# Four layers on one core: row maxima in two halves, and the causal mask of the scores moved from TensorE to GpSimd

## The chip, the core and the metric

The kernel runs on one core of a Trainium2 chip. The metric is the device time of one execution in microseconds; a time of several runs is their median. The core has five engines that take their instructions in order and wait for each other through semaphores: PE is TensorE (matrix products into eight PSUM banks), DVE is VectorE, ACT is ScalarE, POOL is GpSimd, and SP issues transfers.

## The reference, cut to what matters

Sixteen batches of 512 tokens with 128 channels go through four layers, each followed by a residual sum and a layer norm: an RWKV block, a soft decision tree, causal attention with 16 heads of 8 channels, and a mixture of 16 experts. The change is in the attention:

```python
scores = jnp.einsum('bthd,bshd->bhts', q, k) / jnp.sqrt(jnp.float32(dh))
causal = jnp.triu(jnp.full((seq, seq), -jnp.inf, dtype=jnp.float32), k=1)
scores = scores + causal[None, None, :, :]
weights = jax.nn.softmax(scores, axis=-1)
out = jnp.einsum('bhts,bshd->bthd', weights, v).reshape(b, seq, d)
return out @ Wo
```

A token t attends to the keys s up to t. The softmax subtracts each row's maximum before the exponential.

## The kernel before

**Stages.** The batches run through the layers as a pipeline. Each engine has a hand-written list of steps, ORDER, with entries such as `3:score0`: in turn t the step score0 is done for batch t - 3. An engine goes through its list once a turn, so the lists set where every step stands, and nothing reorders them later. One turn brings one batch in and one out, each in another layer; 16 batches and lags of up to 5 make 21 turns, of which the first and last are partly empty.

**Attention of a batch.** The scores are computed twice. First by rows (steps row0 to row39, tokens in the partitions): a unit is 512 columns in one of two banks, S[0] and S[1], and VectorE takes the maxima of it (rowmax, lines 743 and 746). A pair of heads makes five units. After all 40 units four small steps (max_parts, lines 751 to 757) split the negated maxima into three bf16 parts, TensorE turns them (maxT) in bank G, ScalarE copies them (maxT_out), and one transfer (max_rows on SP) puts them as three more rows beside the queries qh. Then come the scores transposed (score0 to score39, keys in the partitions), in the same two banks; their product includes the subtraction of the maximum. ScalarE takes the exponentials into prob (exp0 to exp39), a ring of ten units, and TensorE weighs the values with them (weigh0 to weigh15, four for ten units). pvT_out, back, attend, attT and attn_out end the attention; routing and experts follow. weigh waits for exponentials (semaphore prob), exp of a unit waits until weigh has freed its place in the ring.

**The mask.** Both computations see whole blocks of 128 tokens only as far as the diagonal. On the diagonal block itself a second matmul with the identity adds -1e30 where a key is later than its token: maskb by rows, maskTb in the transposed scores, 64 of each per batch:

```python
mm(to, kh[:, h, i * P:(i + 1) * P], qh[:, h, i * P:T], True, False, skip_group_check=True)
last = mm(to[:, 0:P], identb[:, :], maskTb[:, :], False, True, skip_group_check=True)
```

**Around it.** In the same turn VectorE does the RWKV scans and reciprocals (line 693) of another batch. There, GpSimd has per chunk a weight sum wk (line 386), r_sig (390), gated (395) and rwkv (400), and TensorE the products k, v and r; four read_outs then end in x2 on VectorE (703). GpSimd also has roots of the norms (352 to 360), sums and parts of the rotated heads (rope_sum 418, rest 422, part_lo 428), whose transfers (heads) the next batch's row0 waits for, and half of the gated expert inputs (u, 444). In the trace nearly every matmul has line 925, the helper mm.

Of the kernel before, what the change touches and what calls it, by code (L numbers as in the profile page):

```python
# [23 lines left out]
PARTS = 3  # L24
KROWS = PARTS * PARTS * DH
# [8 lines left out]

LNS = (0, 1, 2, 3, 4, 6, 7)
# [9 lines left out]
    row_ps=UNITS, rowmax=UNITS, max_part=4, maxT_ps=1, maxT=1, max_in=16, score_ps=UNITS, prob=UNITS, pv=16, pvT=2, back_ps=2, pv_inv=2, att=2,  # L45
# [6 lines left out]
        2:heads0 2:heads1 1:shared_bias 0:load 2:max_rows 4:store  # L52
    """,
    pool="""
        2:part_lo0 1:rwkv3 2:rope_sum1 2:rest1 0:root0 2:part_lo1 1:root2 0:x1_gain 0:x1_bias 2:root4 4:root7 3:root6 1:res 0:root1 1:cmr_sig
        1:cmr_sum 3:gate_rest 3:gate_lo 3:u1 1:root3 3:u3 3:u5 0:wk0 3:u7 3:u9 3:u11 0:r_sig0 3:u13 3:u15 0:r_sig1 0:gated0 0:rwkv0 0:r_sig2 0:wk1
        0:wk2 0:gated1 1:root_rms 0:gated2 0:rwkv1 0:r_sig3 0:gated3 1:rope_sum0 0:wk3 1:rest0 0:rwkv2
    """,
    act="""
        2:mix_before4 2:cmk_tanh0 5:norm7 2:cmk_tanh1 4:norm6 2:cmk_tanh2 4:xdT_out 2:cmk_tanh3 4:route_exp 3:values 2:cmr_tanh 1:norm1 3:norm4  # L60
        4:gate_hi 4:gate_mid 4:gT_out 1:mix_before0 1:mix_before1 4:spread1 1:mix_before2 4:spread3 4:spread5 2:norm3 1:k_exp0 4:spread7 2:xbT_out
        1:k_first0 4:spread9 1:r_tanh0 4:spread11 2:gate0 2:gate1 4:spread13 3:vaug 4:spread15 1:r_tanh1 3:maxT_out 1:k_exp1 1:k_exp2 3:exp0 3:exp1
        1:k_first1 3:exp2 3:exp3 1:r_tanh2 3:exp4 3:exp5 3:exp6 3:exp7 2:leafT_out0 3:exp8 3:exp9 2:leafT_out1 3:exp10 1:k_first2 3:exp11 3:exp12
        3:exp13 1:k_exp3 3:exp14 3:exp15 3:exp16 3:exp17 2:norm_rms 3:exp18 3:exp19 2:xcT_out 1:r_tanh3 3:exp20 3:exp21 1:k_first3 3:exp22 3:exp23
        3:exp24 3:exp25 2:part_hi0 3:exp26 3:exp27 3:exp28 2:part_mid0 3:exp29 3:exp30 3:exp31 3:exp32 3:exp33 2:part_hi1 3:exp34 3:exp35 3:pvT_out0
        2:part_mid1 3:exp36 3:exp37 1:weights 3:exp38 3:exp39 0:norm0 3:pvT_out1 1:norm2 3:attT_out 1:mix_before3
    """,
    dve="""
        4:route_probs 3:rowmax10 4:largest0 4:others 3:rowmax11 3:rowmax12 4:largest1 4:gates 3:rowmax13 3:rowmax14 2:y0 3:rowmax15 3:rowmax16 4:u0
        3:rowmax17 2:moments3 4:u2 3:rowmax18 3:rowmax19 1:mix0 1:mix1 1:mix2 4:u4 3:rowmax20 3:rowmax21 1:clamp0 3:rowmax22 4:u6 3:rowmax23  # L70
        3:rowmax24 1:ksum0 3:rowmax25 3:rowmax26 3:rowmax27 4:u8 3:rowmax28 3:rowmax29 1:kv0 3:rowmax30 3:rowmax31 4:u10 3:rowmax32 3:rowmax33
        1:kvsum0 3:rowmax34 4:u12 3:rowmax35 1:clamp1 2:tree0 3:rowmax36 1:wkv0 3:rowmax37 3:rowmax38 4:u14 3:rowmax39 2:tree1 3:max_parts 2:tree2
        2:tree3 1:inverse0 1:kv1 1:clamp2 2:tree4 2:tree5 2:tree6 2:tree7 1:kvsum1 4:yd 1:ksum1 1:wkv1 1:kv2 1:clamp3 1:kvsum2 1:ksum2 1:wkv2 2:yb
        2:moments4 1:inverse1 1:ksum3 1:kv3 1:kvsum3 2:rope_mul0 1:wkv3 2:rope_mul1 1:inverse2 1:inverse3 2:rope_mul2 2:rope_mul3 0:moments0
        4:moments7 1:x2 1:weights 1:moments2 3:attend0 3:attend1 2:rowmax0 2:rowmax1 0:moments1 2:rowmax2 3:yc 1:mix3 3:moments6 1:mix4 2:rowmax3
# [10 lines left out]
        1:cmk0 1:cmk1 2:row5 2:row6 1:cmk2 2:row7 2:row8 3:xdT 1:cmk3 3:centroids 2:row9 1:cmr 2:row10 3:shared 1:cmv0 2:row11 2:row12 1:cmv1 2:row13
        1:cmv2 2:row14 1:cmv3 2:row15 3:gT 2:row16 0:xnT 3:gb0 2:row17 3:biases 3:gb1 3:expert0 3:gb2 2:row18 2:row19 3:gb3 3:expert1 3:gb4 2:row20
        2:row21 3:expert2 0:v0 0:k0 3:gb5 2:row22 3:expert3 3:gb6 2:row23 2:row24 3:expert4 3:gb7 2:row25 1:xbT 2:row26 3:gb8 0:r0 2:row27 3:expert5
        2:row28 2:row29 3:gb9 3:expert6 2:row30 2:row31 3:gb10 1:gates0 2:row32 3:expert7 2:row33 3:gb11 2:row34
# [4 lines left out]
def build(nc: bass.Bass, a, out):  # L94
    with ExitStack() as ctx:
# [52 lines left out]
        maskb, maskTb = sb("maskb", [P, P], BF16), sb("maskTb", [P, P], BF16)  # L148
# [146 lines left out]
        def _(sp):  # L295
# [39 lines left out]
            run("sp", {"load": lambda b: load(b + 1) if b + 1 < B else None, **each("heads", 2, spread_heads), "max_rows": spread_maxima, "store": store, "shared_bias": shared_bias})  # L335
            until(sp, B - 1, "stored")


        @block.gpsimd
        def _(pool):  # L340
# [576 lines left out]
        def _(pe):  # L917
# [317 lines left out]
```

## Time and profile before

| | before |
|---|---|
| median of 3 runs | 1767.74 us (1767.66 to 1773.95) |
| the profiled execution, its own time | 1774.35 us |
| its span, first to last instruction | 1772.6 us |
| mean granted TensorE clock | 0.962 of full speed |
| busy in the span: PE, DVE, ACT, POOL | 90%, 82%, 57%, 51% |
| busy in a steady turn of 98.70 us: PE, DVE, ACT, POOL | 95.81, 89.99, 61.98, 55.40 us |

The clock is full from 226 us to 1650 us after the trace's first event and changes between its two levels before and after. A busy PE is not PE at its peak, since matmuls overlap: the step from the start of one matmul to the start of the next tells what one costs in a row of them.

### The profile page before, as it was taken

How to read it: one execution, taken by the hardware profiler on the slowest of the kernel's cores; microseconds unless marked ns; L12 is line 12 of the kernel's file. 1: busy time of each engine (PE TensorE's matmuls, PEld its weight loads, DVE VectorE, ACT ScalarE, POOL GpSimd, SP SyncE). 2: the span in 40 equal slices, each digit the busy share in tenths (PEclk: the TensorE clock that was granted, in tenths of full speed). 3: DMA queues.
4: the chain of work that ended last, by engine and by line, in shares of the span. 5: the costliest groups of instructions: out<-in, count | busy, mean ns of one | idle time of the engine just before them, and what ended most of it. 6: DMA issues, size and time to landing. Idle time of an engine off the chain costs nothing.

```text
span 1772.6 us, 33600 instructions
## 1 busy us (share of the span) xinstructions
PE 1599.3 (90%) x12064; PEld 1073.9 (61%) x12141; DVE 1460.7 (82%) x3386; ACT 1004.2 (57%) x1998; POOL 898.4 (51%) x1120
## 2 busy tenths in 40 slices
PE   4367799999999999999999999999999999998876
PEld 1235357576666757576666767575757667574635
DVE  5677879899898989898998989898998989783702
ACT  3233474857656574757566574747566575736251
POOL 6435274646456464746555464736465564632202
PEclk9687899999999999999999999999999999999887
DMA  4001010100102020101102010101101020101000
GB/s 108 0 6 54 8 55 9 36 25 22 47 9 61 8 55 14 46 16 30 40 10 59 8 54 15 54 8 39 30 17 52 8 55 8 55 9 50 12 7 7
DMA packets 66921, 53.35 MB, mean 30 GB/s; under 512 B 8322, under 2 KB 65474, under 8 KB 66754
## 3 DMA queue, kind: packets, MB, share of 16 engines
q1 hardware_dynamic: 65602, 50.41, 10.3%
q8 instruction: 96, 1.57, 0.4%
q10 hardware_dynamic: 1152, 0.79, 0.1%
q14 instruction: 71, 0.58, 0.1%
HBM read 8.44 MB, written 4.19 MB: 7 GB/s over the span
## 4 chain that ended last, share of the span: by engine, by line
PE 69%; DVE 22%; ACT 3%; issue 3%; DMA 1%; POOL 1%; SPq 0%; ACTq 0%; DVEq 0%; POOLq 0%
PE bank L925 65%; DVE rmax L746 6%; PE bank L921 4%; DVE stats L645 2%; DVE rmax L743 2%; DVE mixed L654 1%; DVE inner L654 1%; DVE prob L826 1%; DVE mv L650 1%; DVE wkb L693 1%; DMA qh<-maxT 1%; ACT rth L498 1%; ACT prob L498 1%; ACT pvT L498 1%; DVE xc L776 1%
## 5 line engine op out<-in xcount | busy, mean ns | idle before, releaser
L498 ACT ACTIVATE prob<-bank 128x512 f32<-128x512 f32 x640 | 353.8, 595 | 122.3 <-PE bank L925 114.5
L746 DVE TENSOR_REDUCE rmax<-bank 128x1 f32<-128x512 f32 (+2 forms) x768 | 353.0, 502 | 11.8 <-PE bank L925 11.3
L444 POOL TENSOR_TENSOR prob<-xdT,spread 128x512 f32<-128x512 f32 x128 | 172.7, 1349 | 251.9 <-ACT spread L498 208.7
L925 PE MATMUL bank<-kh,qh 72*128 72x512 bf16 (+3 forms) x1024 | 257.0, 305 | 20.6 <-DVE rmax L746 11.0
L925 PE MATMUL bank<-wexpT,prob 128*128 128x128 f32 x2048 | 271.6, 280 | 1.0
L925 PEld LDWEIGHTS bank<-wexpT,prob 128*128 128x128 f32 x2048 | 254.9, 194 | 19.8 <-issue 12.4
L925 PE MATMUL bank<-qh,kh 75*128 75x512 bf16 (+3 forms) x1024 | 246.2, 304 | 10.9 <-ACT prob L498 5.7
L498 ACT ACTIVATE spread<-bank 128x512 f32<-128x512 f32 x128 | 76.4, 597 | 255.5 <-PE bank L925 127.7
L693 DVE RECIPROCAL wkb<-wkb 128x512 f32<-128x512 f32 x64 | 211.6, 3327 | 0.0
L925 PE MATMUL bank<-maskb,identb 128*128 128x128 bf16 x1024 | 191.8, 222 | 0.0
L925 PE MATMUL bank<-maskTb,identb 128*128 128x128 bf16 x1024 | 190.8, 221 | 0.0
L925 PEld LDWEIGHTS bank<-qh,kh 75*128 75x128 bf16 x1024 | 100.1, 98 | 148.5 <-ACT prob L498 95.3
L925 PE MATMUL bank<-prob,vaug 128*32 128x512 f32 (+3 forms) x2048 | 175.8, 445 | 0.0
L925 PEld LDWEIGHTS bank<-kh,qh 72*128 72x128 bf16 x1024 | 102.6, 100 | 90.9 <-DVE rmax L746 44.2
L386 POOL TENSOR_TENSOR wkb<-wkb,ksum 128x512 f32<-128x512 f32 x64 | 88.6, 1384 | 133.9 <-DVE ksum L680 74.0
L498 ACT ACTIVATE rth<-bank 128x512 f32<-128x512 f32 x128 | 76.1, 594 | 87.4 <-PE bank L925 73.5
L925 PEld LDWEIGHTS bank<-maskb,identb 128*128 128x128 bf16 x1024 | 101.9, 100 | 32.9 <-issue 13.7
L925 PEld LDWEIGHTS bank<-maskTb,identb 128*128 128x128 bf16 x1024 | 101.2, 99 | 29.5 <-issue 26.8
L356 POOL TENSOR_TENSOR rstd<-var,exponent 128x4 f32<-128x4 f32 x112 | 113.5, 1013 | 1.3
L826 DVE TENSOR_TENSOR prob<-xdT,bank 128x512 f32<-128x512 f32 x128 | 86.5, 676 | 27.1 <-PE bank L925 23.9
L400 POOL TENSOR_TENSOR inner<-rth,wkb 128x512 f32<-128x512 f32 x64 | 95.4, 1490 | 15.4 <-DVE wkb L693 13.6
L390 POOL TENSOR_SCALAR rth<-rth 128x512 f32<-128x512 f32 x64 | 50.6, 790 | 88.0 <-ACT rth L498 88.0
(210 smaller groups left out, 3288.1 us busy)
## 6 DMA issues: line engine op xcount, KB each, us to landing
qh<-part SPq DMA_DIRECT2D x288, 64.0 KB
kh<-part SPq DMA_DIRECT2D x288, 64.0 KB
x<-in_L_attn_x_dram SPq DMA_DIRECT2D x16, 256.0 KB, 3.0
out_dram<-yo SPq DMA_DIRECT2D x16, 256.0 KB, 3.2
qh<-maxT SPq DMA_DIRECT2D x16, 48.0 KB
wk<-in_L_attn_tm_Wk_dram ACTq DMA_DIRECT2D x1, 256.0 KB, 5.9
wv<-in_L_attn_tm_Wv_dram ACTq DMA_DIRECT2D x1, 256.0 KB, 6.2
wr<-in_L_attn_tm_Wr_dram ACTq DMA_DIRECT2D x1, 256.0 KB, 6.4
```

Of the source, the lines that this page charges most:

```text
L356: raised(pool.tensor_tensor(rstd[:, n, :], var[:, n, :], exponent[:, :], ALU.pow), f"root{n}")
L386: raised(pool.tensor_tensor(wkb[:, c % 2, :], wkb[:, c % 2, :], ksum[:, c % 2, 0:T], ALU.add), "wk")
L390: raised(pool.tensor_scalar(rth[:, c % 2, :], rth[:, c % 2, :], 0.5, 0.5, ALU.mult, ALU.add), "r_sig")
L400: raised(pool.tensor_tensor(inner[:, c, :], rth[:, c % 2, :], wkb[:, c % 2, :], ALU.mult), "rwkv")
L444: raised(pool.tensor_tensor(ug[:, e % 4, :], xdT[:, :], spread[e // 2 % 2][:, :], ALU.mult), "ug_side")
L498: raised(act.activation(dst, src, func, **kw), signal)
L645: last = dve.bn_stats(stats[:, n, j, :], t[:, j, :])
L693: raised(dve.reciprocal(wkb[:, c % 2, :], wkb[:, c % 2, :]), "wk_inv")
L746: last = dve.tensor_reduce(rmax[:, j, h:h + 1], S[n % 2][:, col:col + (j + 1) * P], AX_X, ALU.max)
L826: raised(dve.tensor_tensor(ug[:, e % 4, :], xdT[:, :], G, ALU.mult), "ug")
L921: last = pe.transpose(bk[:, j * P:(j + 1) * P], t[:, j, :], ident[:, :])
L925: return pe.matmul(out_, w, x, start=start, stop=stop, **kw)
```

## The change

The masks on the transposed scores go, with maskTb. The exponentials of the diagonal blocks are taken of unmasked scores, and a new GpSimd step, cut, overwrites those of later keys with zeros in place: for each pair of heads one AFFINE_SELECT over four diagonal blocks, one over two, and, after the pair's fifth unit, one over two more. weigh waits for cut instead of prob. The maxima are split, turned, copied and transferred in two halves of eight heads. The first half borrows S[0] after row unit 24; row unit 26 waits for its copy. score20 to score39 wait for the second half, which uses G as before. The order lists of all engines are new.

```diff
+HALF_MAX = PARTS * NH // 2
+FREED_FOR_MAXIMA = 24
...
-        2:heads0 2:heads1 1:shared_bias 0:load 2:max_rows 4:store
+        2:heads0 2:heads1 1:shared_bias 0:load 2:max_rows0 2:max_rows1 4:store
...
+        2:cut10 2:cut11 1:rope_sum1 0:gated3 0:rwkv2 0:rwkv3 1:rest1 2:cut12
...
-            def spread_maxima(b):
-                until(sp, b, "maxT")
-                sp.dma_start(qh[KROWS:KALL, :, :], maxT[:, :]).then_inc(sems["max_in"], 16)
+            def spread_maxima(b, z):
+                until(sp, b, "maxT", z + 1)
+                sp.dma_start(qh[KROWS:KALL, z * NH // 2:(z + 1) * NH // 2, :], maxT[:, :]).then_inc(sems["max_in"], 16)
...
-                if e == NE - 1 and b + 1 < B:
-                    until(pool, b + 1, "max_part")
...
+            def cut_later_keys(b, k):
+
+                pair, last = k // 2, k % 2
+                first = 5 * (pair % 2)
+                until(pool, b, "prob", 5 * pair + 4 + last)
+                diagonals = [prob[:, first + 4, :].rearrange("p (n s) -> p n s", n=2)[:, :, 0:P]] if last else [prob[:, first:first + 4, 0:P], prob[:, first + 1:first + 4:2, 3 * P:]]
+                for t in diagonals:
+                    raised(pool.affine_select(out=t, in_=t, compare_op=ALU.is_ge, fill=0.0, base=0, pattern=[[0, t.shape[1]], [1, P]], channel_multiplier=-1), "cut")
...
-            def max_parts(b):
-                until(dve, b, "rowmax")
+            def max_parts(b, z):
+
+                heads = slice(z * NH // 2, (z + 1) * NH // 2)
+                to, of, left, done = max_part[z], rmax[:, :, heads], max_rest[:, :, heads], 4 * z
+                until(dve, b, "rowmax", (z + 1) * UNITS // 2)
+                if z == 0:
+                    until(dve, b - 1, "maxT_ps")
...
-                if n >= 2:
+                if n == FREED_FOR_MAXIMA + 2:
+                    until(pe, b, "maxT", 1)
+                elif n >= 2:
                     until(pe, b, "rowmax", n - 1)
...
+                for j in range(J):
+                    last = mm((S[0], G)[z][:, j * P:(j + 1) * P], max_cols[z][:, j * HALF_MAX:j * HALF_MAX + P], identb[:, :])
                 raised(last, "maxT_ps")
...
-                if n == 0:
-                    until(pe, b, "max_in")
+                if n in (0, UNITS // 2):
+                    until(pe, b, "max_in", 16 if n == 0 else 32)
...
-                    mm(to, kh[:, h, i * P:(i + 1) * P], qh[:, h, i * P:T], True, False, skip_group_check=True)
-                    last = mm(to[:, 0:P], identb[:, :], maskTb[:, :], False, True, skip_group_check=True)
+                    last = mm(to, kh[:, h, i * P:(i + 1) * P], qh[:, h, i * P:T], skip_group_check=True)
                 raised(last, "score_ps")
...
-                until(pe, b, "prob", 10 * g + (8, 9, 9, 10)[step])
+                until(pe, b, "cut", 6 * g + (5, 5, 5, 6)[step])
```

On TensorE, around the first score, a steady turn of the kernel before has the following; the turning of the maxima, a product k and three more experts stand right ahead of it. wexpT are expert products, qh with kh the scores, mixed with wr an RWKV product.

```order
L925 MATMUL bank<-wexpT,prob 128x128 [waits s_ug_side]
L925 MATMUL bank<-wexpT,prob 128x128 x3
L925 MATMUL bank<-qh,kh 128x512 [waits s_rowmax,s_max_in]
L925 MATMUL bank<-maskTb,identb 128x128
L925 MATMUL bank<-qh,kh 128x384
L925 MATMUL bank<-maskTb,identb 128x128
L925 MATMUL bank<-qh,kh 128x128
L925 MATMUL bank<-maskTb,identb 128x128
L925 MATMUL bank<-mixed,wr 128x512 [waits s_k_min]
L925 MATMUL bank<-qh,kh 128x512 [waits s_prob]
L925 MATMUL bank<-maskTb,identb 128x128
```

The changed kernel has there:

```order
L942 MATMUL bank<-wexpT,prob 128x128 [waits s_ug_side]
L942 MATMUL bank<-wexpT,prob 128x128 x3
L942 MATMUL bank<-qh,kh 128x512 [waits s_rowmax,s_max_in]
L942 MATMUL bank<-qh,kh 128x384
L942 MATMUL bank<-qh,kh 128x128
L938 MATMUL bank<-ident,tree 128x128 [waits s_gate,s_leaf]
L938 MATMUL bank<-ident,tree 128x128 x3
L942 MATMUL bank<-qh,kh 128x512 [waits s_prob]
```

The masks are gone. The turning of the maxima no longer stands between rows and scores: its first half stands in the row part, behind row25, and its second behind score5.

On GpSimd, in the middle of the scoring part, the kernel before has these steps one behind the other (inner is rwkv, rth is r_sig or gated, tree the rotary sums and rests, part the last part of the heads):

```order
L400 TENSOR_TENSOR inner<-rth,wkb 128x512 [waits s_gated,s_wk_inv]
L390 TENSOR_SCALAR rth<-rth 128x512 [waits s_r_tanh]
L395 TENSOR_TENSOR rth<-rth,kvb 128x512 [waits s_r_sig,s_wkv]
L418 TENSOR_TENSOR tree<-tree 128x512 [waits s_rope_mul]
L386 TENSOR_TENSOR wkb<-wkb,ksum 128x512 [waits s_k_first,s_k_sum]
L422 TENSOR_TENSOR tree<-tree,part 128x512 [waits s_part1]
```

The changed kernel has from the second rwkv on:

```order
L405 TENSOR_TENSOR inner<-rth,wkb 128x512 [waits s_gated,s_wk_inv]
L456 AFFINE_SELECT prob<-prob 128x2x128 [waits s_prob]
L456 AFFINE_SELECT prob<-prob 128x4x128 [waits s_prob]
L456 AFFINE_SELECT prob<-prob 128x2x128
L456 AFFINE_SELECT prob<-prob 128x2x128 [waits s_prob]
L400 TENSOR_TENSOR rth<-rth,kvb 128x512 [waits s_r_sig,s_wkv]
L423 TENSOR_TENSOR tree<-tree 128x512 [waits s_rope_mul]
L391 TENSOR_TENSOR wkb<-wkb,ksum 128x512 [waits s_k_first,s_k_sum]
L427 TENSOR_TENSOR tree<-tree,part 128x512 [waits s_part1]
```

The 24 selects of a batch stand in this queue, each waiting for exponentials, with all that follows behind them.

## Rows read from the trace of the kernel before

**Rows 1.** The page, part 1: busy us, share, instructions.
```profile
PE 1599.3 (90%) x12064; PEld 1073.9 (61%) x12141; DVE 1460.7 (82%) x3386; ACT 1004.2 (57%) x1998; POOL 898.4 (51%) x1120
```

**Rows 2.** Timeline of ScalarE: start us, us, what, [idle before <-releaser].
```profile
800.15 0.59 ACT L498 ACTIVATE maxT<-bank 48x512 bf16<-48x512 f32 x1 [0.52 <-PE bank L925]
...
898.85 0.59 ACT L498 ACTIVATE maxT<-bank 48x512 bf16<-48x512 f32 x1 [0.52 <-PE bank L925]
```

**Rows 3.** Tile maxT: count, ns min/median/max, first and last start.
```profile
L498 ACT ACTIVATE maxT<-bank x16: 590/590/591, 205.0 to 1678.1; 48x512 bf16<-48x512 f32 x16
```

**Rows 4.** Windows of a turn: window: length, busy PE, PEld, DVE, ACT, POOL.
```profile
800.20:898.90 98.70, 95.81 (x753) 65.45 (x757) 89.99 (x210) 61.98 (x124) 55.40 (x69) 1.00 0.11 31
844.20:871.60 27.40, 24.84 (x190) 18.57 (x192) 25.18 (x81) 17.94 (x39) 13.43 (x24) 1.00 0.20 55
871.60:903.20 31.60, 31.38 (x224) 24.62 (x227) 30.73 (x62) 11.51 (x22) 15.99 (x17) 1.00 0.04 11
903.20:942.90 39.70, 39.61 (x339) 22.30 (x338) 34.09 (x68) 32.52 (x64) 25.96 (x29) 1.00 0.12 31
```

**Rows 5.** The chain, 838 to 875 us: start, us, what.
```profile
845.56 0.27 DVE pvi L765
...
871.65 3.49 PE bank L925 x25
```

**Rows 6.** Timeline of VectorE around x2 and attend.
```profile
840.72 0.69 DVE L703 TENSOR_TENSOR x<-x,bank 128x512 f32<-128x512 f32 x1 [3.50 <-PE bank L925]
841.44 0.87 DVE L645 BATCH_NORM_STATS2 stats<-x 128x6 f32<-128x128 f32 x4
...
843.12 0.69 DVE L770 TENSOR_TENSOR att<-bank,pvi 128x128 f32<-128x128 f32 x3
845.56 0.26 DVE L765 RECIPROCAL pvi<-bank 128x16 f32<-128x16 f32 x1 [1.75 <-PE bank L921]
```

**Rows 7.** Waits of VectorE in the turn: total us, times, longest.
```profile
DVE tree L737 <- PE bank L925: 0.6, 2, 0.4
```

**Rows 8.** Tile maskTb.
```profile
L925 PE MATMUL bank<-maskTb,identb x1024: 218/220/315, 209.7 to 1714.3; 128*128 128x128 bf16 x171
...
L473 POOL TENSOR_SCALAR_AFFINE_SELECT maskTb<-maskTb x1: 292/292/292, 20.1 to 20.1; 128x128 bf16<-128x128 bf16 x1
```

**Rows 9.** Timeline of TensorE, a score with its mask and the next.
```profile
903.43 0.22 PE L925 MATMUL bank<-maskTb,identb 128*128 128x128 bf16 x1
903.50 0.33 PE L925 MATMUL bank<-qh,kh 75*128 75x384 bf16 x1
```

**Rows 10.** Tile max_cols in the turn.
```profile
L757 DVE TENSOR_TENSOR max_cols<-max_rest,max_cols x1: 225/225/225, 897.6 to 897.6; 128x64 bf16<-128x64 f32 x1
```

**Rows 11.** Tile rth.
```profile
L390 POOL TENSOR_SCALAR rth<-rth x64: 608/717/1537, 30.2 to 1515.5; 128x512 f32<-128x512 f32 x64
```

**Rows 12.** Groups of GpSimd, 903.2 to 942.9 us: busy us, mean ns, idle before.
```profile
L386 POOL TENSOR_TENSOR wkb<-wkb,ksum 128x512 f32<-128x512 f32 x3 | 4.3, 1431 | 4.0 <-DVE ksum L680 4.0
L395 POOL TENSOR_TENSOR rth<-rth,kvb 128x512 f32<-128x512 f32 x3 | 3.8, 1273 | 1.3 <-DVE kvb L654 1.3
...
L356 POOL TENSOR_TENSOR rstd<-var,exponent 128x4 f32<-128x4 f32 x2 | 2.0, 1016 | 0.0
...
L360 POOL TENSOR_TENSOR shift<-minus,rstd 128x4 f32<-128x4 f32 x1 | 0.2, 203 | 0.1
```

**Rows 13.** Timeline of ScalarE, the exponentials 3 and 4 and the last two.
```profile
905.37 1.08 ACT L498 ACTIVATE prob<-bank 128x512 f32<-128x512 f32 x2
...
940.22 1.08 ACT L498 ACTIVATE prob<-bank 128x512 f32<-128x512 f32 x2 [0.91 <-PE bank L925]
```

**Rows 14.** Timeline of GpSimd, the last rwkv of a turn.
```profile
932.52 1.28 POOL L400 TENSOR_TENSOR inner<-rth,wkb 128x512 f32<-128x512 f32 x1 [0.20 <-DVE wkb L693]
```

**Rows 15.** Timeline of TensorE, the first read_out and the score behind it.
```profile
934.62 1.11 PE L925 MATMUL bank<-wo,inner 128*128 128x128 f32 x8
935.56 0.38 PE L925 MATMUL bank<-qh,kh 75*128 75x512 bf16 x1
```

More of the change, by code:

```diff
@@ L61 @@
[L61 to L64, printed above, removed]
@@ L72 @@
[L72 to L75, printed above, removed]
@@ L86 @@
[L86 to L89, printed above, removed]
+        3:score1 2:leafT0 3:score2 2:leafT1 3:score3 3:score4 1:r2 3:score5 3:maxT1 3:score6 1:v2 3:score7 3:score8 2:leaf_sum 3:score9 3:score10
@@ L90 @@
+        0:k1 3:expert6 2:row30 0:v1 2:row31 3:gb10 3:expert7 2:row32 2:row33 3:gb11 3:expert8 3:gb12 0:r1 3:expert9 2:row34 2:row35 3:gb13 3:expert10
+        3:gb14 3:expert11 0:k2 2:row36 2:row37 3:gb15 3:expert12 2:row38 2:row39 3:expert13 3:expert14 3:expert15 2:score0
     """,
@@ L183, in build @@
         rmax, max_rest = sb("rmax", [P, J, NH]), sb("max_rest", [P, J, NH])
-        max_cols, gate_cols = (sb(n, [P, (J - 1) * PARTS * NH + P], BF16) for n in ("max_cols", "gate_cols"))
-        max_part, gate_part = (t[:, 0:J * PARTS * NH].rearrange("p (j i h) -> p j i h", j=J, i=PARTS) for t in (max_cols, gate_cols))
-        maxT = sb("maxT", [PARTS * NH, T], BF16)
+        gate_cols = sb("gate_cols", [P, (J - 1) * PARTS * NH + P], BF16)
+        gate_part = gate_cols[:, 0:J * PARTS * NH].rearrange("p (j i h) -> p j i h", j=J, i=PARTS)
+        max_cols = [sb(f"max_cols{z}", [P, (J - 1) * HALF_MAX + P], BF16) for z in range(2)]
+        max_part = [t[:, 0:J * HALF_MAX].rearrange("p (j i h) -> p j i h", j=J, i=PARTS) for t in max_cols]
+        maxT = sb("maxT", [HALF_MAX, T], BF16)
         pvT = attT = sb("pvT", [P, T])
@@ L334, in _ @@
             sp.wait_ge(setup["kh_ones"], 4)
-            run("sp", {"load": lambda b: load(b + 1) if b + 1 < B else None, **each("heads", 2, spread_heads), "max_rows": spread_maxima, "store": store, "shared_bias": shared_bias})
+            run("sp", {"load": lambda b: load(b + 1) if b + 1 < B else None, **each("heads", 2, spread_heads), **each("max_rows", 2, spread_maxima), "store": store, "shared_bias": shared_bias})
             until(sp, B - 1, "stored")
@@ L598, in _ @@
                 "values": take_values, "vaug": place_values, **each("part_hi", 2, first_part), **each("part_mid", 2, second_part),
-                "maxT_out": lambda b: move(b, maxT[:, :], G[0:PARTS * NH, :], "maxT_ps", "maxT"),
+                **each("maxT_out", 2, lambda b, z: move(b, maxT[:, :], (S[0], G)[z][0:HALF_MAX, :], "maxT_ps", "maxT", z + 1, freed=[("max_in", 16 * (2 * b + z))])),
                 **each("exp", UNITS, score), **each("pvT_out", 2, weighed),
@@ L838, in _ @@
                 **each("tree", DEPTH, tree), "yb": add_tree, "moments4": lambda b: (until(dve, b, "yb"), moments(b, 4, yb)),
-                **each("rope_mul", 4, rope_product), **each("rowmax", UNITS, row_maxima), "max_parts": max_parts, **each("attend", 2, attended),
+                **each("rope_mul", 4, rope_product), **each("rowmax", UNITS, row_maxima), **each("max_parts", 2, max_parts), **each("attend", 2, attended),
                 "yc": add_attention, "moments6": lambda b: (until(dve, b, "yc"), moments(b, 6, yc[b % 2])),
@@ L1176, in _ @@
                 "xcT": turn_in, **each("rope", 4, rope_product), "attn_v": attention_values,
-                **each("row", UNITS, row_scores), "maxT": turn_maxima, **each("score", UNITS, scores), **each("weigh", 16, weigh),
+                **each("row", UNITS, row_scores), **each("maxT", 2, turn_maxima), **each("score", UNITS, scores), **each("weigh", 16, weigh),
                 **each("back", 2, turn_back), "attT": turn_attention, "attn_out": attention_out, "xdT": turn_experts, "centroids": centroids,
```

91 lines of the change are left out of this document (51 added, 40 removed).

## The prediction

> **What bounds the kernel now.** I read the page first, then the period of the program, then one period stage by stage, then the chain and the waits. The page gives busy shares of 90% for TensorE, 82% for VectorE, 57% for ScalarE and 51% for GpSimd [rows 1]; as averages over filling and draining they name no bound. The copy of the maxima (maxT) occurs once a batch, at 800.15 and 898.85 us, so a steady turn takes 98.70 us [rows 2]; from first to last copy there are 15 turns in 1473.1 us, 98.2 on average [rows 3]. In that turn TensorE is busy 95.81 us and VectorE 89.99 [rows 4]: two engines near their limit, each with its own tight stage. In the maxima part after the attention's tail (844.2 to 871.6) TensorE is busy for 24.84 of 27.40 us; from there on it has almost no gap (31.38 of 31.60, 39.61 of 39.70) [rows 4]. The chain says the same: it is VectorE's from 845.56 to 871.6, TensorE's from there on [rows 5], and TensorE's alone until the end of the attention.
>
> VectorE's idle time in a turn is short and named: 3.5 us before x2 (line 703), waiting for read_out on TensorE, 1.8 before the second half of attend (line 765) [rows 6], and six waits of 0.2 to 0.6 us, 1.9 together; those before the rotary products make the largest entry (0.6 for two) [rows 7]. That is 7.2 us; so of 98.70 us VectorE is occupied for 91.5, its short gaps between dependent instructions included. **This is the number that decides**: whatever TensorE is relieved of, VectorE leaves at most 7.2 us of a turn to win.
>
> **The change, part by part.** *The masks on the scores go.* 64 matmuls of 128 columns a batch (1024 in all). The profile puts 220 ns on each [rows 8], but they are pipelined: in the scoring part the next matmul starts 0.07 us after a mask's start (903.43 to 903.50) [rows 9], and 0.06 at most of the others. 64 x 0.06 = 3.8 us a turn. In the scoring part TensorE has no gap [rows 4], so all of it is on TensorE's path there: 98.70 - 3.8 = 94.9 us, were TensorE alone to decide. Bounds: nothing (if VectorE holds the turn) and 3.8.
>
> *The maxima in two halves.* VectorE does eight small steps instead of four. The old ones take up to 0.225 us on 64 elements [rows 10]; the new ones have 32 and take, I estimate, 0.18 with the wait for the one before: eight make 1.45, the four old ones 0.9. I add 0.6 us a turn (bounds 0.2 and 0.9). One more copy of 0.59 us on ScalarE and one more transfer of half the size lie beside other work: ScalarE is busy for 62 of 98.70 us [rows 4]. What the halves give is freedom: the first scores no longer wait for the chain row39, maximum, four steps, turning, copy, transfer. But TensorE did experts and projections in that gap and did not stand still (31.38 of 31.60) [rows 4], so I book no gain of its own, only that the work can stand elsewhere. Row score 26 now waits for the first half's copy, as their bank is borrowed; two other units of work stand ahead of it, and I book nothing (at worst one copy and its hops, 1 us).
>
> *GpSimd's selects.* For each pair of heads there are three: 512, 256 and 256 elements, 24 a batch. The trace has AFFINE_SELECT on 128 elements only: 292 ns [rows 8]. A plain GpSimd pass, TENSOR_SCALAR on 512, takes 608 at its best [rows 11], and a small step of 4 elements 0.20 us [rows 12]. From 0.20 to 0.608 is 0.8 ns an element, and with that 128 elements give 0.30, just the 292 seen: I take 0.6, 0.4 and 0.4, so 1.4 us a pair and 11 us a turn. Upper bound: 292 for every block of 128, 2.34 a pair, 18.7 a turn. The lower bound is that of 512 at the rate alone, 9 us. The Trainium skill (GPSIMD Engine Reference, section 3.1) has about 1.8 cycles an element for a tight loop, 769 ns on 512; by it, as an estimate, a pair takes 1.54 us and a turn 12.3. No run here shows that figure yet.
>
> *Where the selects stand.* They belong to the scoring part, where GpSimd is busy for 25.96 of 39.70 us [rows 4]. In the new order one weight sum (1.43), one gating (1.27) and one root (a power of 1.02 and three small steps of 0.20) leave this part [rows 12], which leaves 21.6; with 11 it is 32.6 us. The selects can start after the first four exponentials (906.45) and end after the last (941.3): 34.9 us [rows 13]. So GpSimd fits, with 2 us to spare, in a queue that takes its steps in order. The weighing on TensorE now waits for the select: after the last exponential that it needs, two selects (1.0 us) instead of none. TensorE has two to three more scores in hand there, and ScalarE needs 0.54 a score; what is left of the wait, 0.2 to 0.7 us at four places a turn, falls on a TensorE that has just won 3.8 us. I count it as spent slack, not as path. Also behind GpSimd: the last part of the rotated heads (part_lo1) stands behind the select of the seventh pair now, and the next batch's row scores wait for its transfers.
>
> One rule weighs against this step. The row first: the same TENSOR_SCALAR on GpSimd takes 608 ns at best, 717 in the median and up to 1537 [rows 11]. The Trainium skill (SBUF — State Buffer, section Who interferes with whom) says that a VectorE instruction with two inputs in SBUF and a GpSimd instruction that reads SBUF exclude each other on a shared port for a whole instruction. The spread agrees with it. Without the rule the selects cost 11 us; at the median's excess over the best case, 0.11 us each, 24 of them cost 2.6 more, 13.6: then GpSimd needs 35.2 of 34.9 us, no spare time at all, but less over it than the 2.4 us that I find below.
>
> *VectorE after the change.* Occupied: 91.5 + 0.6 = 92.1. Which waits stay? The one before x2: from the end of the last reciprocal the chain is weighted product on GpSimd (1.28 [rows 14]), four read_outs on TensorE (0.94 each, by the start of the first and of the score behind it [rows 15]), three scores between them (0.7, at 0.22 to 0.24 without masks) and 0.4 of hops: 6.1 us. VectorE has beside it a set of moments and attend's first half, which today, after x2, run from 841.44 to 843.81: 2.4 us [rows 6]. 3.7 us stay, about as before. The wait before attend's second half shrinks: two sets of moments (1.2 each), x2 (0.69) and one row maximum now lie beside weighing, copy and turning (3.9), so 0.2 stays. Of the 1.9 us of short waits 1.7 is for TensorE, which is up to 3.8 us earlier; I leave 0.3. Turn: 92.1 + 3.7 + 0.2 + 0.3 = 96.3 us, 2.4 less than now. TensorE needs 94.9 and fits.
>
> **Sum.** 15 turns x 2.4 = 36 us. Ends: in the last batch nothing hides the selects (four waits of up to 1 us), while the masks leave a scoring part in which ScalarE waits for TensorE; I set these against each other. The profiled execution's own time is 1774.35 (span 1772.6); less 36 it is 1738. The median of the runs shown is 1767.74, 6.6 below the profiled one, so I predict **1732 us**. By the Trainium skill's rate above (12.3 us of selects) the sum would be the same, since 21.6 + 12.3 still fits into 34.9.
>
> **Rivals.**
> *More comes back (0.18).* If read_outs follow each other with no score between and the short waits go, the turn is 92.1 + 3.0 = 95.1, close to TensorE's 94.9: 15 x 3.6 = 54, 1714 us. For it: the order is new everywhere. Against: the x2 chain alone needs 5.4 us.
> *VectorE keeps it (0.15).* The short waits stay and x2's too: 92.1 + 3.7 + 0.2 + 1.9 = 97.9, so 15 x 0.8 = 12: 1756 us. For it: in the maxima part VectorE has the chain [rows 5], and the masks removed were not there.
> *GpSimd becomes the bound: slower (0.22).* It decides once its scoring part is over by more than the 2.4 us otherwise won: 21.6 + selects > 34.9 + 2.4, selects above 15.7 us a turn, 0.65 each on average. At 18.7 the part is 40.3 against 34.9: 5.4 too long, the turn 96.3 + 5.4 = 101.7, 15 x 3.0 = 45 slower: 1813. At 15.7 it is even, and so it is with selects of 0.55 and the 2.6 of waiting above. Late selects then show as TensorE waiting at the weighing, late transfers of the heads, and row scores that wait for them. For it: no select of this shape in the trace; against: 292 ns fits the line of a plain pass.
> The forecast itself has 0.45.
>
> **Chances and range.** A measurement of this kernel tells about 0.5% (9 us) from no change: below 1759 is faster, above 1777 slower. Forecast and first rival are faster (0.63), of the second (1756, at the edge) a third: 0.68. The rest of it (0.10) and a fifth of the third are the same: 0.14. Slower: 0.18. For 8 in 10 I cut half of the first rival's lower side and the upper half of the third: 1703 to 1785. The forecast alone would have 1721 to 1748.
>
> **What would show it.** Right: no mask matmuls in the scoring part, AFFINE_SELECT of 512 at about 0.6 us and of 256 at 0.4; a turn, copy to copy of the second half, of 96 to 97 us; VectorE's x2 wait still 3 to 4 us and its wait before line 765 gone; TensorE's busy share of a turn lower by 3 to 4 points, with its gaps at the weighing. Wrong: selects of 0.9 us or more, GpSimd without gaps from the first to the last select, and row scores waiting for the heads' transfers; or a VectorE with hardly any idle time, in a turn below 95.

## The result, and the profile after

The changed kernel takes **1823.72 us** (median of 4 runs, 1820.75 to 1826.93) beside 1769.91 us of the kernel before on the same chip: ratio 1.030, 95% interval 1.028 to 1.032. It is slower by 3%; the prediction was 1732 us, and its range ended at 1785.

The page, busy time per engine and the granted clock, answers to [rows 1]:

```profile
PE 1593.4 (87%) x11104; PEld 1030.0 (56%) x11181; DVE 1483.5 (81%) x3450; ACT 1019.7 (56%) x2014; POOL 1094.6 (60%) x1503
...
PEclk9788899999999999999999999999999999998867
```

TensorE has lost the instructions that it was meant to lose, and its share fell; GpSimd has 196 us more. The tile view of the maxima's copies (from 925 to 1036 us; two second halves and one first) gives the turn, and the windows of one turn show where it grew; the columns are those of [rows 4]:

```profile
L510 ACT ACTIVATE maxT<-bank x3: 573/573/587, 929.6 to 1031.7; 24x512 bf16<-24x512 f32 x3
```
```profile
864.70:920.40 55.70, 53.68 (x388) 40.65 (x394) 54.12 (x150) 31.94 (x65) 27.57 (x40) 1.00 0.10 27
920.40:923.30 2.90, 2.90 (x29) 2.89 (x27) 2.87 (x7) 0.63 (x1) 1.37 (x2) 1.00 0.00 0
923.30:963.80 40.50, 35.99 (x248) 17.94 (x247) 32.16 (x48) 30.53 (x58) 36.49 (x45) 0.96 0.12 32
963.80:966.50 2.70, 2.60 (x36) 1.01 (x35) 2.35 (x13) 0.08 (x2) 2.46 (x7) 1.00 0.36 100
```

From copy to copy it is 102.1 us, where 98.70 stood [rows 2]. The four windows are the row scores, what lies between them and the scores, the scores (first score to last exponential), and the tail. The first three of them in the kernel before, cut at the same steps:

```profile
845.40:895.40 50.00, 47.91 (x360) 36.53 (x363) 48.34 (x126) 25.81 (x54) 23.47 (x35) 1.00 0.10 29
895.40:903.20 7.80, 7.80 (x55) 6.13 (x53) 7.56 (x17) 2.45 (x5) 4.75 (x5) 1.00 0.15 42
903.20:941.30 38.10, 38.10 (x315) 21.68 (x318) 32.89 (x61) 30.98 (x60) 24.64 (x26) 1.00 0.10 28
```

The row part with what lies behind it grew by 0.8 us (57.8 to 58.6), the scoring part by 2.4 (38.1 to 40.5). In the scoring part GpSimd is busy for 36.49 of 40.50 us, where it had 24.64 of 38.10; TensorE, which had no gap there, now has 4.5 us of them. How GpSimd goes through this part, its timeline shows:

```profile
925.97 1.27 POOL L400 TENSOR_TENSOR rth<-rth,kvb 128x512 f32<-128x512 f32 x1 [4.20 <-DVE kvb L666]
927.20 1.09 POOL L391 TENSOR_TENSOR wkb<-wkb,ksum 128x512 f32<-128x512 f32 x1
928.25 3.23 POOL L456 TENSOR_SCALAR_AFFINE_SELECT prob<-prob 128x512 f32<-128x512 f32 x5
...
946.81 1.16 POOL L427 TENSOR_TENSOR tree<-tree,part 128x512 f32<-128x512 f32 x1
947.92 2.28 POOL L456 TENSOR_SCALAR_AFFINE_SELECT prob<-prob 128x512 f32<-128x512 f32 x3
950.17 0.61 POOL L395 TENSOR_SCALAR rth<-rth 128x512 f32<-128x512 f32 x1
950.75 1.58 POOL L433 TENSOR_TENSOR part<-tree,part 128x512 bf16<-128x512 f32 x1
952.30 1.35 POOL L456 TENSOR_SCALAR_AFFINE_SELECT prob<-prob 128x512 f32<-128x512 f32 x3
```

GpSimd waits 4.2 us for VectorE's kvb, 2.7 of them inside the part. That wait is over at 925.97, before the first four exponentials are done (926.42) and any select could start. From then on it runs with almost no gap to the end of the part: a row without a bracket shows no wait. The timelines of ScalarE and TensorE at the third weighing show what such a queue does to them:

```profile
949.08 2.17 ACT L510 ACTIVATE prob<-bank 128x512 f32<-128x512 f32 x4
954.54 0.60 ACT L510 ACTIVATE prob<-bank 128x512 f32<-128x512 f32 x1 [3.29 <-PE bank L942]
```
```profile
950.81 0.88 PE L942 MATMUL bank<-qh,kh 75*128 75x512 bf16 x3 [0.20 <-ACT prob L510]
953.34 2.75 PE L942 MATMUL bank<-prob,vaug 128*32 128x512 f32 x24 [1.65 <-POOL prob L456]
```

The exponentials end at 951.25. Their select stands in the queue behind a pass on r_sig and a part of the rotated heads, starts at 952.30, and TensorE's weighing starts at 953.34, after a wait of 1.65 us. The scores of the next two units are done by 951.70, but there are ten slots for exponentials, and the next ten cannot run ahead of the weighing that frees them: ScalarE has nothing to do for 3.29 us and goes on at 954.54, when the first of these weighings has ended (954.41). Exponential, select, weighing, next exponential is a closed ring.

The groups of GpSimd by shape give the selects' durations (busy us, mean ns, idle before), and the tile view their spread (min/median/max):

```profile
L456 POOL TENSOR_SCALAR_AFFINE_SELECT prob<-prob 128x256 f32<-128x256 f32 x256 | 139.5, 558 | 7.3 <-ACT prob L510 7.3
...
L456 POOL TENSOR_SCALAR_AFFINE_SELECT prob<-prob 128x512 f32<-128x512 f32 x128 | 100.7, 787 | 44.1 <-ACT prob L510 43.8
```
```profile
L456 POOL TENSOR_SCALAR_AFFINE_SELECT prob<-prob x384: 398/410/1565, 212.3 to 1764.4; 128x256 f32<-128x256 f32 x128, 128x512 f32<-128x512 f32 x64
```

The spread has two levels, and the single records of the trace tell them apart. 314 of the 384 selects take 0.63 to 0.65 or 0.40 to 0.42 us. The other 70, the same five of 24 in fourteen batches, take 1.08 to 1.57, and they make up nearly all that the means have over the least. Each of these 70 starts while a VectorE instruction with two inputs in SBUF is running (a scan in 56 cases) and ends after it; none of the 314 starts so. One of the 70, and the scan:

```profile
937.70 1.33 POOL L456 TENSOR_SCALAR_AFFINE_SELECT prob<-prob 128x256 f32<-128x256 f32 x1
```
```profile
937.53 1.30 DVE L697 TENSOR_TENSOR_SCAN kvsum<-decay,kvb 128x512 f32<-128x512 f32 x1
```

### The profile page after: what moved, and what is told of

Read it like the earlier page. It is cut to its first block, busy times and chain, and to the rows that moved or that the text cites. A ratio compares the mean times of both kernels' runs of the same rounds, so it can differ in the third digit from the quotient of the medians.

```text
span 1824.8 us, 32237 instructions
## 1 busy us (share of the span) xinstructions
PE 1593.4 (87%) x11104; PEld 1030.0 (56%) x11181; DVE 1483.5 (81%) x3450; ACT 1019.7 (56%) x2014; POOL 1094.6 (60%) x1503
## 4 chain that ended last, share of the span: by engine, by line
PE 42%; DVE 20%; POOL 17%; issue 11%; ACT 7%; DMA 1%; SPq 1%; ACTq 0%; POOLq 0%; DVEq 0%
PE bank L942 41%; POOL prob L456 7%; DVE rmax L758 6%; ACT prob L510 3%; DVE stats L657 2%; POOL inner L405 2%; DVE inner L666 2%; PE bank L938 1%; POOL rth L395 1%; DVE mixed L666 1%; POOL rth L400 1%; POOL tree L423 1%; POOL wkb L391 1%; DVE mv L662 1%; DVE prob L843 1%
## 5 line engine op out<-in xcount | busy, mean ns | idle before, releaser
L942 PEld LDWEIGHTS bank<-wexpT,prob 128*128 128x128 f32 x2048 | 264.9, 193 | 24.0 <-issue 18.7
L942 PE MATMUL bank<-wexpT,prob 128*128 128x128 f32 x2048 | 267.3, 276 | 1.9 <-issue 0.2
L456 POOL TENSOR_SCALAR_AFFINE_SELECT prob<-prob 128x256 f32<-128x256 f32 (+1 forms) x384 | 232.2, 634 | 51.4 <-ACT prob L510 51.1
L942 PE MATMUL bank<-qh,kh 75*128 75x512 bf16 (+3 forms) x1024 | 233.5, 310 | 33.3 <-ACT prob L510 20.9
L942 PE MATMUL bank<-prob,vaug 128*32 128x512 f32 (+3 forms) x2048 | 189.2, 506 | 40.5 <-POOL prob L456 40.5
L942 PEld LDWEIGHTS bank<-qh,kh 75*128 75x128 bf16 x1024 | 82.0, 98 | 207.9 <-ACT prob L510 161.9
L400 POOL TENSOR_TENSOR rth<-rth,kvb 128x512 f32<-128x512 f32 x64 | 81.5, 1273 | 137.9 <-DVE kvb L666 95.1
L942 PEld LDWEIGHTS bank<-prob,vaug 128*32 128x32 f32 x2048 | 61.5, 121 | 149.2 <-POOL prob L456 75.5
L395 POOL TENSOR_SCALAR rth<-rth 128x512 f32<-128x512 f32 x64 | 40.6, 635 | 99.2 <-ACT rth L510 99.2
L692 DVE TENSOR_TENSOR_SCAN ksum<-decay,kk 128x512 f32<-128x512 f32 x64 | 84.4, 1319 | 16.3 <-ACT kk L510 16.3
```

Source lines behind the costliest of these rows:

```text
L395: raised(pool.tensor_scalar(rth[:, c % 2, :], rth[:, c % 2, :], 0.5, 0.5, ALU.mult, ALU.add), "r_sig")
L400: raised(pool.tensor_tensor(rth[:, c % 2, :], rth[:, c % 2, :], kvb[:, c % 2, :], ALU.mult), "gated")
L456: raised(pool.affine_select(out=t, in_=t, compare_op=ALU.is_ge, fill=0.0, base=0, pattern=[[0, t.shape[1]], [1, P]], channel_multiplier=-1 ...
L692: raised(dve.tensor_tensor_scan(ksum[:, c % 2, 1:T + 1], decay[:, c:c + 1].broadcast_to([P, T]), kk[:, c % 2, :], 0.0, ALU.mult, ALU.add), ...
L942: return pe.matmul(out_, w, x, start=start, stop=stop, **kw)
```

## The experiments

Theory 1: the selects fill GpSimd's queue in the scoring part and lengthen it. Theory 2: the new order, whose row part is 5.7 us longer, costs the time. Theory 4: taking masks off TensorE is worth nothing, as VectorE holds the turn. Theory 3: VectorE's work makes selects longer, and this decides. That 70 of 384 are longer beside it, the records above show; how much of the time hangs on that was not tried by a kernel of its own. All times are medians; 1772 to 1773 us is the kernel before on the same chip. "Turn" is the mean of the 15 steady turns, the start of the last copy of the maxima (second halves, where they are halved) less that of the first; beside it stands, where there is one, what most of those turns take whose windows show a granted clock of 1.00, the level of 2.4 GHz (in the kernel before 98.7, in the changed kernel, where only two turns have it, 101.0).

**First group: take the parts away one by one.**

*No selects* (the cut steps also leave GpSimd's list), new order and halves kept:
```
-  until(pe, b, "cut", 6 * g + (5, 5, 5, 6)[step])
+  until(pe, b, "prob", 10 * g + (8, 9, 9, 10)[step])
```


> The changed kernel without any of its selects; the weighing waits for the exponentials, as before. Left out: the masking of the transposed scores. The new order and the halved maxima stay. Theory 1 (the selects fill GpSimd's queue in the scoring part, and the weighing and the rotated heads behind them lengthen it): the scoring part falls from 40.6 to about 35 us, GpSimd has gaps there again, the turn falls from 102 to 96 or 97, the time to 1725 to 1745 us. Theory 2 (the new order costs the time, the row part above all, which grew from 50.0 to 55.7 us; the selects are beside the path): the turn stays above 101, the time at 1805 to 1825. Something between, 1760 to 1790, would share the loss among them.

*Narrow selects*, same places and waits:
```
-  for t in diagonals:
-      raised(pool.affine_select(out=t, in_=t, compare_op=ALU.is_ge, fill=0.0, base=0, pattern=[[0, t.shape[1]], [1, P]], channel_multiplier=-1), "cut")
+  for t in [d[:, :, 0:4] for d in diagonals]:
+      raised(pool.affine_select(out=t, in_=t, compare_op=ALU.is_ge, fill=0.0, base=0, pattern=[[0, t.shape[1]], [1, 4]], channel_multiplier=-1), "cut")
```


> The changed kernel with each select cut to 4 columns of its blocks: the same number of selects, in the same places, with the same waits, but with 16 and 8 elements in place of 512 and 256. Left out: most of the masking of the transposed scores. Theory 1 with the time of the selects as the cause: a small GpSimd step takes 0.2 to 0.3 us, so 24 of them take 5 to 7 us instead of 14.5; GpSimd's part is then 27 to 29 us, fits, and the time is near that of the kernel without selects, 1730 to 1755 us. Theory 1 with the wait itself as the cause (one engine more between exponential and weighing): 1790 to 1820. Theory 2: 1805 to 1825.

*Masks back on TensorE*, no selects, new order and halves:
```
...
+  mm(to[:, 0:P], identb[:, :], maskTb[:, :], False, True, skip_group_check=True)
...
```


> The changed kernel without selects and with the 64 mask matmuls a batch back on TensorE: new order and halved maxima alone, the whole computation. Theory 1: TensorE has 3.8 us a turn more than without masks, so the turn is 98 to 100, the time 1755 to 1785 us. Theory 2: over 1815, as the order costs it and TensorE has more to do. If it is under 1760, the order with the halves is worth something by itself.

*The kernel before without masks on the scores*:
```
...
-  last = mm(to[:, 0:P], identb[:, :], maskTb[:, :], False, True, skip_group_check=True)
```


> The kernel before, in its old order and with whole maxima, without the mask matmuls of the transposed scores. Left out: the masking of the transposed scores. What the masks alone are worth on TensorE's path: by the prediction's 0.06 us each at most 3.8 us of a turn of 98.7, 1711 us; if VectorE keeps the turn (theory 4), 1755 to 1768 us; with part of VectorE's short waits kept, 1725 to 1745.

| kernel | us | ratio to before (95%) | turn, mean | at 1.00 |
|---|---|---|---|---|
| no selects | 1757.1 | 0.991 (0.989 to 0.993) | 97.0 | 96.9 |
| narrow selects | 1756.7 | 0.991 (0.988 to 0.994) | 97.0 | 97.2 |
| masks back | 1775.6 | 1.002 (1.001 to 1.003) | 98.7 | 99.5 |
| before, no masks | 1752.7 | 0.989 (0.986 to 0.992) | 97.1 | 97.0 |

So the order with the halves costs 3.5 us of the whole time (0.8 of a turn at 1.00: 99.5 beside 98.7), the masks are worth 18.5 in the new order (1775.6 to 1757.1) and 19.4 in the old, and the selects cost 66.6 (1757.1 to 1823.7). Theory 2 falls: the longer row part is all but paid for by a stretch between rows and scores of 2.9 us, where it was 7.8. Theory 4, that the masks are worth nothing, falls too, but the prize was half of what was forecast. (The mean holds the last two turns, which are some 5 us shorter in every kernel.) The narrow selects have all the waits and cost nothing that the time shows, so it is the selects' time, not one engine more in the way. The times of the first two lie above the 1725 to 1745 and the 1730 to 1755 that theory 1 had named, and the last, 1752.7, lies in none of its ranges, just under theory 4's 1755 to 1768. Two scoring parts of the kernel without selects, and one of that with masks back, say why:

```profile
501.60:539.00 37.40, 35.86 (x248) 18.11 (x247) 31.07 (x48) 30.32 (x58) 25.74 (x27) 0.95 0.13 35
797.40:832.90 35.50, 34.08 (x247) 17.65 (x245) 31.01 (x47) 30.18 (x58) 25.69 (x27) 1.00 0.13 36
```
```profile
903.70:941.80 38.10, 37.41 (x311) 21.89 (x309) 31.88 (x47) 30.48 (x58) 26.01 (x28) 1.00 0.13 35
```

At a granted clock of 1.00 (2.4 GHz) the 64 masks are worth 38.1 - 35.5 = 2.6 us, not 3.8: TensorE is busy for 3.3 us less, and its gaps grow from 0.7 to 1.4. (In the old order a turn falls from 98.7 to 97.0, by 1.7.) And in other turns of the same run the clock is 0.95 over the part, some of it at the lower level of 1.2 GHz, and the part is 37.4 us: six of the first thirteen turns have a mean clock of 0.98 and take 98.2 to 98.9 us beside 96.9. With the masks every steady part had 1.00.

**Second group: how much fits.** First the selects twice (each done again in its place), then the passes on r_sig moved to ScalarE, then half the selects (even pairs of heads; the wait stands in weigh, beside that for prob), in the new and in the old order:

```
...
+  for t in [t for t in diagonals for _ in range(2)]:
...
```
```
...
-  raised(pool.tensor_scalar(rth[:, c % 2, :], rth[:, c % 2, :], 0.5, 0.5, ALU.mult, ALU.add), "r_sig")
+  move(b, rth[:, c % 2, :], rth[:, c % 2, :], "r_tanh", "r_sig", c + 1, scale=0.5, bias=half_one[:, 0:1])
...
```
```
...
+  cut = n // 5 % 2 == 0
+  if not cut:
+      last = mm(to[:, 0:P], identb[:, :], maskTb[:, :], False, True, skip_group_check=True)
...
+  until(pe, b, "cut", 3 * g + 3)
```


> The changed kernel with every select done twice in its place, 48 a batch. Theory 1 (GpSimd is full from the first select of a batch to its last, so that each further microsecond there is a microsecond of the turn): 14 to 15 us more a turn, 116 to 117 us, a time of 2010 to 2060 us. A theory of partial cover (part of the selects lies in gaps that GpSimd still has): 4 to 8 us more a turn, 1885 to 1945. Theory 2 (order): about 1825 to 1840.

> The changed kernel with all its selects, but the four passes x0.5+0.5 of r_sig a batch, 0.62 us each at best, on ScalarE in place of GpSimd. Two of the four stand between a batch's first select and its last. Theory 1: the turn is shorter by these two, 1.2 to 1.6 us, that is 1798 to 1808 us, at most by all four, 2.5 us, 1786. If it is not GpSimd's time as such that counts but the selects' own waits, 1820 to 1827.

> The whole computation in the new order, with half the selects: those of the even pairs of heads on GpSimd, masks on TensorE for the odd pairs. Theory 1: GpSimd needs 25.7 + 7.2 = 33 us in a scoring part of 36 to 37 and fits, so the time lies midway between the order with masks (1775.6) and the order without masks or selects (1757.1): 1760 to 1772 us. If selects cost in proportion to their number whether they fit or not, half of 67 us more: 1795 to 1805.

> The whole computation in the order of before, with whole maxima, and half the selects: the even pairs of heads, put where GpSimd had gaps (11 us of gaps in the old scoring part, 7.2 us of selects); masks on TensorE for the odd pairs. Theory 1: they fit, and the time is midway between before (1772) and before without masks (1753): 1758 to 1768 us, faster than both kernels. If they don't fit there either: 1780 to 1800.

Selects twice: 2007.8 us (one run), just below theory 1's 2010 to 2060. r_sig on ScalarE: 1819.9, a miss for theory 1 (1798 to 1808), at the edge of the other reading (1820 to 1827). Half in the new order: **1763.9, ratio 0.996 (0.995 to 0.997)**, as theory 1 had it. Half in the old order: 1815.1, a plain miss.

The last two differ in nothing but order and halves. In the old order my places for the selects were gaps of GpSimd, but gaps in which it waited for a result that others need next. A select that stands there waits for its exponentials and holds up the weight sums behind it. VectorE's reciprocals, which never waited before, then do (group rows of the kernel before and of this one, idle before and releaser at the end):

```profile
L693 DVE RECIPROCAL wkb<-wkb 128x512 f32<-128x512 f32 x64 | 211.6, 3327 | 0.0
```
```profile
L703 DVE RECIPROCAL wkb<-wkb 128x512 f32<-128x512 f32 x64 | 213.6, 3340 | 30.1 <-POOL wkb L386 30.1
```

30.1 us over the run, 1.9 a turn; how much of the 42 us beside the kernel before this alone makes was not tried.

**Third group: sum or place?** The miss with r_sig left two readings, so one kernel leaves these passes out altogether, and one changes a place and no work:

```
...
-  2:cut8 2:cut9 0:r_sig3 1:part_lo0 2:cut10 2:cut11 1:rope_sum1
+  2:cut8 2:cut9 2:cut10 2:cut11 0:r_sig3 1:part_lo0 1:rope_sum1
...
```


> The changed kernel with two steps of GpSimd's list earlier: the selects of the sixth pair of heads stand ahead of a pass on r_sig and a part of the rotated heads (0.61 and 1.58 us in the changed kernel), no longer behind them. GpSimd's work is the same. If the loss lies in the ring from exponential to select to weighing to the next exponentials, so that what stands ahead of a select in the queue counts: the third weighing starts 1.0 to 1.5 us earlier, 15 turns, 1802 to 1812 us. If only the sum of GpSimd's work counts (full from first select to last): no change, 1818 to 1828 us.

> The changed kernel with the four passes on r_sig a batch left out altogether (they are neither on GpSimd nor on ScalarE). Left out: the factor 0.5 and the summand 0.5 of the receptance. If the sum of GpSimd's work from first select to last counts: 1.2 to 1.6 us a turn less, 1798 to 1808 us. If a select's own way from exponential to weighing counts, whatever else GpSimd has to do: 0.3 us a turn or less, 1816 to 1826. The kernel with these passes on ScalarE gained 4 us, but its exponentials stood behind them there; if that was what cost it the rest, this one is 8 to 15 us faster than that.

Without the passes: 1803.4 us, 20 less, 1.4 a turn, as the sum of GpSimd's work has it; of that 1.0 at the clock of 1.00, where a turn takes 100.0 us and one of the changed kernel 101.0. The passes on ScalarE gave only 4. The waits of TensorE for exponentials and for selects (total us, times, longest), first with the passes on ScalarE, then with none:

```profile
PE bank L941 <- ACT prob L506: 33.0, 88, 0.8
PE bank L941 <- POOL prob L452: 25.2, 39, 1.7
```
```profile
PE bank L938 <- POOL prob L452: 25.8, 43, 1.7
...
PE bank L938 <- ACT prob L506: 21.3, 78, 0.6
```

TensorE waits for selects alike in both, and 11.7 us longer for exponentials where ScalarE has the passes: the moved work holds up the exponentials there, as far as these waits tell.

Selects first: 1827.8 us, no gain over 1823.7. The third weighing did what it should, TensorE's wait before it is 0.18 us in place of 1.65:

```profile
953.21 1.93 PE L942 MATMUL bank<-prob,vaug 128*32 128x512 f32 x24 [0.18 <-POOL prob L456]
```

Over the run TensorE's waits for selects fall from 40.5 to 19.6 us, but those for exponentials rise from 20.9 to 33.9. And two turns of this kernel, then two of the changed one, copy to copy, say that this run answers less than was asked:

```profile
726.10:829.70 103.60, 97.04 (x700) 64.62 (x699) 91.06 (x214) 63.25 (x126) 67.50 (x93) 0.97 0.11 29
829.70:930.90 101.20, 95.86 (x699) 62.44 (x699) 90.99 (x214) 63.14 (x125) 67.36 (x93) 0.98 0.11 30
```
```profile
317.80:420.50 102.70, 96.00 (x695) 62.60 (x699) 91.49 (x214) 63.21 (x126) 67.97 (x93) 0.97 0.10 27
827.70:929.60 101.90, 95.19 (x694) 62.58 (x699) 91.50 (x214) 63.20 (x126) 67.88 (x93) 0.98 0.11 30
```

At a granted clock of 0.98 over the turn the moved selects are worth 0.7 us, half of the 1.0 to 1.5 expected from the place. At 0.97, which every second turn was granted, the turn takes 103.6 and one of the changed kernel 102.7, so that it loses 0.9. Whether the place counts stays open; that the sum counts, the kernel without the passes shows (1.0 at the clock of 1.00). What made the clock fall in every second turn was not tried.

**Last: a little more than half.** In the new order, half the selects and those of the last unit of each odd pair (`cut = n // 5 % 2 == 0 or n % 5 == 4`).

> The whole computation in the new order with half the selects, as the version that was faster than before, and four more a batch: those of the last unit of the odd pairs too (0.41 us each, needed only by the last of four weighings). 24 masks a batch stay on TensorE in place of 32. If GpSimd still has room, TensorE's 8 masks are worth 0.3 to 0.5 us a turn: 1756 to 1761 us. If GpSimd's part is full at this point already, 1.6 us more of selects show: 1766 to 1780.

1772.3 us, ratio 1.000 (0.999 to 1.001): more than half is too much already. The table has the selects' time by the group rows, over 16 batches, and what they cost a turn at 1.00: the turn, less 96.9, less 2.6 x (masks left / 64), which takes the worth of the masks to be in proportion to their number.

| selects | us a turn on GpSimd | masks left | turn, mean | at 1.00 | cost of the selects |
|---|---|---|---|---|---|
| none | 0 | 0 | 97.0 | 96.9 | 0 |
| narrow | 6.6 | 0 | 97.0 | 97.2 | 0.3 |
| half | 8.0 | 32 | 97.8 | 98.6 | 0.4 |
| five eighths | 9.6 | 24 | 98.3 | 98.9 | 1.0 |
| all | 14.5 | 0 | 101.1 | 101.0 | 4.1 |
| all twice | 25.5 | 0 | 113.2 | none | |

Up to 8 us they are nearly free, at 9.6 they begin to cost, and from all to twice 11.0 us more on GpSimd make 12.1 of the turn (part of that is clock: none of its steady turns had 1.00). In the new order half the selects take 0.9 us from a turn (99.5 to 98.6), but beside the kernel before (98.7) almost nothing: of the 8 us between the two profiled executions, five lie in the first and the last two turns.

## Why the prediction was wrong

**The step that failed is "GpSimd fits, with 2 us to spare".** It set 32.6 us of work against 34.9 between the first four exponentials and the last. Two terms were off. This stretch in the kernel before, in the one without selects and in the changed one, all at a granted clock of 1.00:

```profile
906.40:941.30 34.90, 34.90 (x299) 20.02 (x300) 29.93 (x54) 27.78 (x55) 24.57 (x25) 1.00 0.11 30
```
```profile
800.40:832.90 32.50, 31.14 (x228) 15.95 (x228) 28.11 (x41) 27.57 (x54) 25.30 (x27) 1.00 0.15 40
```
```profile
417.30:453.80 36.50, 31.84 (x228) 15.84 (x228) 29.18 (x41) 27.65 (x54) 35.85 (x45) 1.00 0.12 34
```

*The stretch*: 34.9 us hold with the masks on TensorE. I let the turn shrink by 2.4 without them, but not the stretch; it is 32.5, and by my own prices nothing was to spare. *The selects*: the base price was right (0.63 and 0.40 us at their least, 0.6 and 0.4 taken), but the means are 0.79 and 0.56, so they keep GpSimd busy for 14.5 us a turn and not 11. The port rule that I weighed (Trainium skill, SBUF — State Buffer, Who interferes with whom) agrees with the 70 long selects, each beside a VectorE instruction with two inputs in SBUF. Its 0.11 us each was the excess of a median; here the median is near the least (637 and 408 ns), and the means lie 0.16 above the least, 3.8 us a turn, nearly all of it from the 70. No run here took the overlap away. The rate for a tight loop (Trainium skill, GPSIMD Engine Reference, section 3.1: 769 ns on 512) is above what 100 of the 128 selects of 512 took, 0.63 to 0.65.

What else GpSimd had to do was sized well: 21.6 us, and 21.4 are seen (35.85 less 14.5). So 35.9 us of work met a stretch of 32.5. With 0.65 us of gaps the stretch is 36.5, 4.0 longer, and the turn 4.1 (96.9 to 101.0): this is the whole cost of the selects.

**"I count it as spent slack, not as path"** failed with it. The weighing's wait was priced at 0.2 to 0.7 us at four places, 0.8 to 2.8 a turn. It was 1.65 at one place and 2.5 a turn over the run (TensorE's matmuls waited 40.5 us for selects): the size was right, but it lies on the path, since the exponentials cannot go on ahead of it with ten slots. No run had more slots.

**The masks** had the right mechanism and too large a size: 2.6 us a turn at the full clock for 3.8, and 18.5 us of the whole time, where a gain of 36 rested on them. In six of the first thirteen turns without selects the clock took back 1.3 to 2.0 of the 2.6: the same part was 37.4 us at 0.95.

**VectorE's floor held**: 96.3 us forecast; the turn of the kernel without selects is 96.9 where the clock stays at 1.00, with the x2 wait at 3.85 us (3.7 forecast). The wait before the second half of attend, for which 0.2 was left, is gone; instead 0.76 us stand before its first half. With all selects these are 3.33 us, since the weighing is late. The **halves** were booked at 0.6 us a turn and the **order** at nothing; together they cost 0.8 at the full clock, 3.5 us in all, ratio 1.002. VectorE's two waits in the kernel without selects, and the one that grew in the changed kernel:

```profile
828.18 0.48 DVE L781 RECIPROCAL pvi<-bank 128x16 f32<-128x16 f32 x3 [0.76 <-PE bank L937]
...
833.23 0.69 DVE L714 TENSOR_TENSOR x<-x,bank 128x512 f32<-128x512 f32 x1 [3.85 <-PE bank L941]
```
```profile
959.06 0.48 DVE L782 RECIPROCAL pvi<-bank 128x16 f32<-128x16 f32 x3 [3.33 <-PE bank L938]
```

**The third rival was the mechanism**, GpSimd as the bound with waits at the weighing. Its point of decision, 15.7 us of selects, adds the 2.4 won to the 34.9, though winning them shortens the stretch: with 21.6 of other work 34.9 are full, and the turn as long as before, at 13.3. At 14.5 the time was already above the 1813 that it gave for 18.7. Had the selects taken 11 us as priced, a straight line between the table's rows of 9.6 and 14.5 would give them a cost of 1.9 (an estimate), a turn of 98.8 beside the 98.7 of before: no change. So the forecast's sign, too, rested on room that was not there. (The lower bound of 9 us for the selects does not follow from its rate: 0.8 ns for each of 1024 elements in eight pairs is 6.6, and 608 ns for each 512 of them 9.7. Nothing rests on it.)

## What to carry to other kernels

An engine's idle time in a stretch is not room for new work. Measure the stretch as the change will leave it (32.5 us here, not 34.9), and set the new work in it at its mean duration beside the other engines, not at its best. A gap that is a wait for an operand holds new work only if nothing behind it is held up, as the half in the old order was. Ask of a step that is put between a producer and its consumer how many buffers lie around it; with a ring of ten slots the wait comes round to the producer. When part of a move fits for nothing, do that part: half the selects gave 0.4% where all of them lost 3% (0.7% beside the same order with all masks, 1775.6 to 1763.9).

## What the hardware showed that I had not expected

A GpSimd AFFINE_SELECT started beside a running VectorE scan took 1.3 us where it took 0.40 by itself, and the same five of 24 were hit in fourteen of sixteen batches. This also draws up the means of the narrow selects (399 and 244 ns): 55 of the 384 take 0.49 to 1.15 us. Their medians are 227 ns for 16 elements in four blocks and 194 for 8, beside 637 and 408 for 512 and 256, so a select costs some 0.2 us and 0.8 to 0.9 ns an element (an estimate from these four), close to the line of the prediction. Their tile view (min/median/max over both sizes):

```profile
L456 POOL TENSOR_SCALAR_AFFINE_SELECT prob<-prob x384: 185/195/1149, 211.1 to 1698.1; 128x8 f32<-128x8 f32 x128, 128x16 f32<-128x16 f32 x64
```

And work taken off TensorE cost it some of its clock: with masks every steady scoring part was granted 1.00; without them TensorE was busy for 34.08 of 35.50 us instead of 37.41 of 38.10, and six of the first thirteen turns had parts at 0.95, up to 1.9 us longer for the same matmuls. What in the gaps brings the clock down was not tried.
